# Second attention one step earlier: the next tile's projections and relay move forward by a step, and the first half's logits go in front of the second half's transposes

## The chip, the core and the metric

One core of a Trainium2 chip runs the whole program: TensorE (PE; its weight loads are listed apart as PEld), VectorE (DVE), ScalarE (ACT), GpSimd (POOL) and SyncE (SP), and 16 DMA engines that all queues share. The metric is the device time of one execution in microseconds (us), lower is better; a few runs are taken and their median is compared. The span is the part of an execution that the hardware profiler covers.

## The reference, cut to what matters

Two layers on 1024 tokens of width 512. Each is an attention, a residual with layer norm, a feed-forward part, and again a residual with layer norm. The change touches the second attention and the start of the last feed-forward part (its expert logits).

```python
x = _layernorm(x + _L0_attn_ref(x, ...))            # attention over the heads of one token
x = _layernorm(x + _L0_ffn_ref(x, ...))             # three layers of +1/-1 weights
# _L1_attn_ref: 32 heads of 16, a window of 128 keys, rotary embedding
q = (x @ Wq.T).reshape(B, S, 32, 16); k = _split_kv(x @ Wk.T); v = _split_kv(x @ Wv.T)
q = q * cos + rotate_half(q) * sin
k = k * cos + rotate_half(k) * sin
scores = einsum('bhqd,bhkd->bhqk', q, k) / 4
scores = where((j <= i) & (j > i - 128), scores, -inf)
out = einsum('bhqk,bhkd->bhqd', softmax(scores), v)
x = _layernorm(x + out @ Wo.T)
# _L1_ffn_ref: the top 2 of 16 experts by these logits, and a shared expert
logits = x2 @ gate_w.T
x = _layernorm(x + moe_out + shared_out)
```

## The kernel before, in words

Five programs, one per engine, are written out by hand and run in order on their engines; semaphores tie them together. The 1024 tokens are 8 tiles of 128. A float32 product is made of three matmuls of rounded halves (`split_terms`), so a projection of one tile is 12 matmuls with 512 columns.

**PSUM rings.** `Ring` (line 46) hands out banks in a fixed order: `fill` waits until the bank's former content has been released, `take` and `drained` wait for a filling and for its release. In the second attention V (two banks) holds the scores by rows, Q (two) the scores by keys, R (two) the projections and the output product, and U has one bank alone (line 213) for everything that is transposed in between: x2 (the input), turned (rotated K or Q), mx (the row maxima), context2 and co. So each filling of U waits until the one before it has been read by its last reader.

**The second attention** is a loop over i from -1 to 7 with eight steps s each. At step s three tiles are in work: r = i+1 has its scores by rows made on PE (`row_scores`) and their masked maxima taken on VectorE (`row_maxima`, four instructions of line 1184 per step); i has its scores by keys made (`key_scores`), exponentiated on ScalarE (`weights_out`), masked on GpSimd (`mask`, lines 1818 and 1821) and weighed with the values on PE (`weigh`, line 601); and t = i+2 is projected. d = i-1 gets its context transposed (`context_rows`, line 546), divided (`context_divided`), transposed again (`turn_context`, line 553) and multiplied with the output weights (`output`, in thirds at steps 5, 6 and 7), and `add_output` adds it to X.

**The projections of tile t before the change.** Step 0: K (`project2(t, 1)`, twelve matmuls of line 515). Step 1: Q, then the maxima of tile i's second half of heads are transposed (`turn_maxima(i, 1)`, line 539); VectorE in that step takes the row maxima, divides the context, rotates K (`rotate` and `rope_sum`, line 914), and then copies the maxima out (`maxima_out`). Step 2: the rotated K is transposed (`turn_rotated(t, 1)`, line 533), a third of V is made, and VectorE rotates Q. Step 3: the rest of V, and the rotated Q is transposed. Step 6: the input of the next tile is transposed (`turn_x`, line 508).

**The relay.** `parts_out_high` (ScalarE) and `parts_low` (VectorE) make the two rounded parts of rotated K and Q; SyncE writes them to DRAM (`relay_rows`, line 865) and GpSimd loads them back in another layout (`stack_rows`, line 1803, K in step 4 and Q in step 5). `row_scores(r, 0)` waits for both loads of tile r. `stack_maxima` (line 1810) puts the maxima beside them by a DMA, and `key_scores(i, 0, 0)` waits for it. After the last tile's relay SyncE loads the first shared-expert weights (`load_shared`, line 853), two of 768 KB, and a table.

**The passage.** After the loop the last tile's output is made, the tiles are normalised on ScalarE (`normalise`), transposed on PE (`turn_x3`, V ring, line 343), split by ScalarE and VectorE (`high_x3`, `low_x3`), and multiplied with the gate weights in two halves of four tiles (12 matmuls of line 332 each), copied out on VectorE (line 1314), and turned to logits by tokens, on which the choice of experts rests. The shared expert's products follow.

```python
                    if s < 2 and 2 <= t < T:
                        project2(t, 1 - s)
                    if s == 1 and i >= 0:
                        turn_maxima(i, 1)
```

Of the kernel before, what the change touches and what calls it, by code (L numbers as in the profile page):

```python
# [16 lines left out]
D = 512  # L17
DC = D // P
T = 1024 // P
G = 4  # L20
# [3 lines left out]
E = 16  # L24
# [55 lines left out]
def build(nc, x, wq, wk, wv, bias, k0, k1, k2, s0, s1, s2, aq, ak, av, ao, gate, experts, shared,  # L80
          rope_c, factor_c, table_c, out, xs, ys):
    with ExitStack() as ctx:
# [81 lines left out]
        co = FP[:, 13440:13952]  # L164
# [163 lines left out]
        def _(pe):  # L328
# [190 lines left out]
            def project2(t, n, at=0, count=3 * DC):  # L519

                if at == 0:
                    U.drained(pe, ("x2", t))
                    if n == 2:
                        pe.wait_ge(w_split, 4)
                    else:
                        pe.wait_ge(kq_split, (8, 4)[n])
                part_of(R, ("qkv", t, n), split_terms(turned_parts(x2T[t]), chunks(wsplit((1, 2, 0).index(n)))), at, count)
# [107 lines left out]
            for i in range(-1, T):  # L635
                t, r, d = i + 2, i + 1, i - 1
                for s in range(8):
# [6 lines left out]
                    if s < 2 and 2 <= t < T:  # L644
                        project2(t, 1 - s)
                    if s == 1 and i >= 0:
                        turn_maxima(i, 1)
                    if s == 2 and 2 <= t < T:
                        turn_rotated(t, 1)
                        project2(t, 2, 0, DC)  # L650
                    if s == 3 and 2 <= t < T:
                        project2(t, 2, DC, 2 * DC)
                        turn_rotated(t, 0)
                    if s == 4 and d >= 0:
                        turn_context(U, U, d)
# [14 lines left out]
                    if s == 6 and 2 <= t < T - 1:  # L670
                        turn_x(t + 1)
                    if s == 7 and d >= 0:
                        output(U, R, d, 2 * DC, DC)
                    if i >= 0 and s in (3, 5, 7):
                        weigh(i, s // 2 - 1)
# [14 lines left out]
            turn_x3(*range(2, T - 1))  # L690


# [3 lines left out]
            for g in range(2):  # L696
                if g == 1:
                    turn_x3(T - 1)
                V.drained(pe, ("x3", g * G + G - 1))
                x3 = [[XT3[g][:, a, c, :] for c in range(DC)] for a in range(2)]  # L700
                b = V.fill(pe, ("logitsT", g))
                product(b[0:E, :], split_terms([[gr[:, a, c, :] for c in range(DC)] for a in range(2)], x3)).then_inc(V.full, 1)
# [201 lines left out]
        def _(v):  # L904
# [343 lines left out]
            for i in range(-1, T):  # L1248
                t, r, d = i + 2, i + 1, i - 1
                for s in range(8):  # L1250
# [4 lines left out]
                    if s == 1 and 2 <= t < T:  # L1255
                        rotate(t, 1)
                        rope_sum(t, 1)
                    if s == 1 and i >= 0:
                        maxima_out(i, 1)
                    if s == 2 and 2 <= t < T:  # L1260
                        parts_low(t, 1)
                        rotate(t, 0)
                        rope_sum(t, 0)
                    if s == 3 and r < T:
                        maxima_split(r, 0)
                    if (i, s) == (-1, 3):
                        low_dense(("x2", 2), xa[2][1], xa[2][0])
                    if s == 3 and 2 <= t < T:
                        parts_low(t, 0)
# [8 lines left out]
                    if s == 6 and 2 <= t < T - 1:  # L1278
                        low_dense(("x2", t + 1), xa[t + 1][1], xa[t + 1][0])
# [21 lines left out]
            nc.vector.memset(picked[:, T, :], 0.0).then_inc(picked_ready, 1)  # L1301
            low_x3(0, 1)
            add_output(R, T - 1)
            low_x3(2, 3, 4)
            rates(slice(T - 1, T), 6)
            low_x3(5, 6)
            shared_low(2)


            for g in range(2):  # L1310
                if g == 1:
                    low_x3(T - 1)
                b = V.take(v, ("logitsT", g))
                nc.vector.tensor_copy(lgT[:, g * D:(g + 1) * D], b[0:E, :]).then_inc(V.free, 1)
# [132 lines left out]
        def _(s):  # L1447
# [190 lines left out]
            for i in range(-1, T):  # L1638
                t, d = i + 2, i - 1
                for step in range(8):  # L1640
                    if step == 0 and d >= 0:
                        context_out(d, 1)
                    if i >= 0 and (step % 2 == 0 or i >= 1):
                        weights_out(i, 2 * (step // 2), step % 2)
                    if step == 2 and 2 <= t < T:
                        parts_out_high(t, 1)
                    if step == 3 and 2 <= t < T:
                        values_out(t, ("qkv", t, 0))
                        parts_out_high(t, 0)
                    if step == 4 and d >= 0:  # L1650
                        high_dense(("co", d), coT[:, 0])
# [13 lines left out]
                    if step == 6 and 2 <= t < T - 1:  # L1665
                        high_dense(("x2", t + 1), x2T[t + 1][:, 0])
# [8 lines left out]
            roots(slice(0, T - 1), 5)  # L1675
            s.wait_ge(offset_ready, 6)
            normalise(0)
            normalise(1)
            high_dense(("co", T - 1), coT[:, 0])
            for t in range(2, T - 1):  # L1680
                normalise(t)
                high_x3(t - 2)
# [3 lines left out]
            high_x3(T - 3)  # L1686
            high_x3(T - 2)
            high_x3(T - 1)
# [38 lines left out]
        def _(p):  # L1727
# [103 lines left out]
            for i in range(-1, T):  # L1831
                t, r = i + 2, i + 1
                for step in range(8):
# [7 lines left out]
                    if step == 2 and i >= 0:  # L1841
                        stack_maxima(i, 1)
                    if step == 4 and 2 <= t < T:
                        stack_rows(t, 1)
                    if step == 5 and 2 <= t < T:
                        stack_rows(t, 0)
# [78 lines left out]
```

## Time and profile before

| what | value |
|---|---|
| three runs | 734.14, 737.02, 726.03 us |
| median of the runs | 734.14 us |
| the profiled execution | 728.87 us |
| its span | 727.1 us |
| mean granted clock of TensorE, share of full speed | 0.911 |
| busy share: PE, PEld, DVE, ACT, POOL | 85, 66, 54, 37, 33% |

The profiled execution took 1.8 us beyond its span and lies 5.3 us under the median of the runs. All times in the rows below are from its span's start. In the timeline's rows the columns are the start, the time until the group's end, the engine, the line, the operation with its target and sources, the count, and in brackets how long the engine sat idle before it and what ended that. "issue" is an idle stretch whose end the profile puts down to nothing it shows; waits on a DMA's semaphore come out so in part.

### The profile page before, as it was taken

The page shows a single profiled execution, that of the slowest core. Times are in us where ns is not written, and L with a number is a line of the kernel's source. Part 1 is how long each engine was busy: PE and PEld are TensorE (multiplying, and loading weights), DVE is VectorE, ACT ScalarE, POOL GpSimd, SP SyncE. Part 2 cuts the span into 40 slices and gives each one's busy share as a digit, 9 for nine tenths or more (in the row PEclk, how much of TensorE's full clock was granted, in tenths as well). Part 3 has the DMA queues.
Part 4 walks back from the last instruction along what each step waited for, and adds up shares of the span by engine and source line. Part 5 has one row for each costly group of instructions (what it writes and reads, how often), then busy time and mean ns, then how long its engine had stood idle before and what let it go on. Part 6 is the DMA issues. An engine that isn't in the chain of part 4 may idle for free.

```text
span 727.1 us, 13453 instructions
## 1 busy us (share of the span) xinstructions
PE 616.0 (85%) x5108; PEld 482.4 (66%) x5108; DVE 393.3 (54%) x1126; ACT 270.3 (37%) x433; POOL 238.9 (33%) x348
## 2 busy tenths in 40 slices
PE   2998999669889787989989895868789799999984
PEld 2987976557667555666767673645458688888761
DVE  4325445697765774757777484552554243323264
ACT  5155045366654223334344342444430122221213
POOL 6002523543410245535444452362007311111071
PEclk9999999889999885999999897577799899999997
DMA  8921211342056425536272648020007759998465
GB/s 293 394 115 31 52 33 26 104 134 74 0 139 150 119 96 81 132 46 159 45 152 89 88 119 156 2 89 2 1 1 283 270 209 416 418 417 292 168 165 182
DMA packets 49455, 104.37 MB, mean 144 GB/s; under 512 B 12208, under 2 KB 18480, under 8 KB 47856
## 3 DMA queue, kind: packets, MB, share of 16 engines
q1 hardware_dynamic: 30032, 61.68, 24.0%
q0 software_dynamic: 13744, 31.61, 19.3%
q10 hardware_dynamic: 5616, 10.23, 3.9%
q8 instruction: 41, 0.67, 0.4%
q14 instruction: 22, 0.18, 0.1%
HBM read 63.77 MB, written 35.13 MB: 136 GB/s over the span
## 4 chain that ended last, share of the span: by engine, by line
PE 62%; DVE 10%; ACT 9%; issue 7%; DMA 7%; POOL 4%; SPq 1%; POOLq 0%; ACTq 0%; DVEq 0%
PE bank L332 20%; PE bank L515 10%; PE bank L368 9%; ACT FP L1451 4%; DVE FP L914 3%; PE bank L601 3%; PE bank L586 3%; PE bank L573 3%; DMA QS<-QS 2%; PE bank L750 2%; POOL FP L1866 2%; PE bank L716 2%; PE bank L391 2%; PE bank L546 1%; PE bank L379 1%
## 5 line engine op out<-in xcount | busy, mean ns | idle before, releaser
L1451 ACT ACTIVATE FP<-bank 128x512 f32<-128x512 f32 (+1 forms) x244 | 138.6, 611 | 311.3 <-PE bank L586 128.6
L1184 DVE CUSTOM_DVE_ANT_0 kraw<-bank,maskb 128x256 bf16<-128x256 f32 (+1 forms) x256 | 88.5, 401 | 58.0 <-PE bank L573 58.0
L515 PE MATMUL bank<-W,XR 128*128 128x512 f32 x348 | 104.1, 444 | 0.2
L332 PE MATMUL bank<-FP 128*128 128x128 f32 x558 | 87.3, 311 | 0.8 <-ACT FP L1451 0.8
L368 PE MATMUL bank<-W,XR 128*128 128x512 f32 x288 | 76.6, 415 | 5.2 <-DVE W L914 5.2
L515 PEld LDWEIGHTS bank<-W,XR 128*128 128x128 f32 x348 | 69.4, 211 | 16.0 <-DVE XR L914 0.8
L1818 POOL TENSOR_SCALAR_AFFINE_SELECT FP<-FP 128x512 f32<-128x512 f32 x64 | 41.4, 669 | 114.8 <-ACT FP L1451 114.8
L368 PEld LDWEIGHTS bank<-W,XR 128*128 128x128 f32 x288 | 63.7, 271 | 11.3 <-DVE W L914 5.6
L332 PEld LDWEIGHTS bank<-FP 128*128 128x128 f32 x558 | 65.1, 192 | 2.8 <-DVE FP L914 1.6
L332 PE MATMUL bank<-RP,W 128*128 128x512 f32 x192 | 48.8, 413 | 5.0 <-issue 2.8
L914 DVE TENSOR_TENSOR FP<-FP,bank 128x128 f32<-128x128 f32 (+1 forms) x39 | 14.4, 369 | 70.5 <-ACT FP L1451 44.9
L332 PEld LDWEIGHTS bank<-RP,W 128*128 128x128 f32 x192 | 37.8, 199 | 14.5 <-issue 5.1
L1821 POOL TENSOR_SCALAR_AFFINE_SELECT FP<-FP 128x512 f32<-128x512 f32 x56 | 38.0, 704 | 24.5 <-ACT FP L1451 24.3
L1774 POOL DMA_DIRECT2D RPF<-FP x64 | 31.6, 501 | 39.7 <-PE bank L404 28.8
L1859 POOL DMA_DIRECT2D FP<-slots_in x31 | 16.7, 540 | 84.7 <-PE bank L716 77.8
L573 PE MATMUL bank<-RP,QS 48*128 48x256 f32 x160 | 23.7, 377 | 21.0 <-issue 10.0
L601 PE MATMUL bank<-FP 128*17 128x128 f32 x960 | 39.5, 318 | 2.1 <-ACT FP L1451 1.8
L1386 DVE COPY FP<-bank 128x512 f32<-128x512 f32 x31 | 21.4, 691 | 33.2 <-PE bank L716 33.2
L914 DVE TENSOR_TENSOR XR<-bank,XR 128x512 fp32r<-128x512 f32 x27 | 21.3, 807 | 32.4 <-ACT XR L1451 32.4
L601 PEld LDWEIGHTS bank<-FP 128*17 128x17 f32 x960 | 27.5, 111 | 14.2 <-issue 6.0
L573 PEld LDWEIGHTS bank<-RP,QS 48*128 48x128 f32 x160 | 14.7, 221 | 32.6 <-issue 23.4
L1854 POOL DMA_INDIRECT slots_in<-X,slots x16 | 16.6, 1037 | 48.6 <-issue 48.6
(168 smaller groups left out, 1019.1 us busy)
## 6 DMA issues: line engine op xcount, KB each, us to landing
FP<-in_experts_dram SPq DMA_DIRECT2D x31, 768.0 KB, 6.6
slots_out<-QS SPq DMA_DIRECT2D x48, 256.0 KB, 2.6
FP<-slots_in POOLq DMA_DIRECT2D x31, 256.0 KB, 6.6
slots_out<-FP ACTq DMA_DIRECT2D x31, 256.0 KB, 7.7
slots_in<-RP SPq DMA_DIRECT2D x7, 1024.0 KB, 13.1
RP<-slots_out POOLq DMA_DIRECT2D x16, 384.0 KB, 5.7
QS<-slots_out POOLq DMA_DIRECT2D x10, 384.0 KB, 8.3
FP<-in_shared_dram SPq DMA_DIRECT2D x4, 768.0 KB, 8.0
```

What stands on the lines that cost most here:

```text
L332: mm = nc.tensor.matmul(bank, lhs, rhs, start=(n == 0), stop=(n == len(terms) - 1))
L368: mm = nc.tensor.matmul(b[:, :], *terms[m], start=(m == 0), stop=(m == 3 * DC - 1))
L515: mm = nc.tensor.matmul(b[:, :], *terms[n], start=(n == 0), stop=(n == len(terms) - 1))
L573: mm = nc.tensor.matmul(both[a][:, m, :], qS[i % 3][half(a, 3 * HD), pr, :], kS[half(a, 3 * HD), slots, pr, :], start=True, stop=True)
L586: mm = nc.tensor.matmul(both[a][:, m * P:(m + 1) * P], kS[half(a, 3 * HD + 2), (i - w) % 4, pr, :], qS[i % 3][half(a, 3 * HD + 2), pr, :], ...
L601: mm = nc.tensor.matmul(weighing[32 * q:32 * q + HD + 1, (h // 4 % 4) * P:(h // 4 % 4 + 1) * P], vaug[:, (i - w) % 4, head(h), :], PT[hg % ...
L914: return nc.vector.tensor_tensor(o, a, b, op)
L1184: ins = nc.vector.tensor_tensor_reduce(masked[:, 2 * (f % 2) + m, 0:n], b[:, m, :], maskb[:, m0:m0 + n], 1.0, -BIG, ALU.add, ALU.max, hmax ...
L1451: return nc.scalar.activation(o, i, func, **kw)
L1774: nc.gpsimd.dma_start(vdiag[k % 3][32 * g:32 * g + 32, 272 * g:272 * g + 272].rearrange("p (s d) -> p s d", s=CH), vT[32 * g:32 * g + 32, ...
L1818: ins = nc.gpsimd.affine_select(out=pt, in_=pt, compare_op=ALU.is_ge, fill=0.0, base=0, pattern=[[0, 4], [1, P]], channel_multiplier=-1)
L1821: ins = nc.gpsimd.affine_select(out=pt, in_=pt, compare_op=ALU.is_ge, fill=0.0, base=-1, pattern=[[0, 4], [-1, P]], channel_multiplier=1)
```

## The change

The loop's iteration count and all operations stay; their order on each engine changes.

- K of the next tile (`project2(t + 1, 1)`) is made in step 7 of the iteration before, behind the output's last third and ahead of `weigh`; Q of tile t in step 0; V in steps 1 and 2; rotated K is transposed in step 1 and rotated Q in step 2; `turn_x(t + 1)` moves from step 6 to step 3.
- `turn_maxima(i, 1)` moves to the end of step 0 on PE. On VectorE `maxima_out(i, 1)` comes in step 0 ahead of `rotate(t, 1)` and `rope_sum(t, 1)`; before it came in step 1 behind them. Rotation of Q and the low parts move one step forward.
- ScalarE: the high parts and V's copy move one step forward, the high part of x2 from step 6 to 3. GpSimd: `stack_rows` in steps 3 and 4, `stack_maxima(i, 1)` in step 1.
- Passage: the logits of the first four tiles come behind the transposes of tiles 2 and 3, and the transposes of tiles 4 to 7 all behind them. On ScalarE the high part of the last context goes ahead of the wait for the offsets, and the high parts of tiles 4 to 7 all behind the last `normalise`. On VectorE the first logits' copy comes ahead of the low parts of tiles 4 to 7, and the second's behind `shared_low(2)`.

```diff
 (TensorE)
-                    if s < 2 and 2 <= t < T:
-                        project2(t, 1 - s)
-                    if s == 1 and i >= 0:
+                    if s == 0 and 2 <= t < T:
+                        project2(t, 0)
+                    if s == 0 and i >= 0:
                         turn_maxima(i, 1)
-                    if s == 2 and 2 <= t < T:
+                    if s == 1 and 2 <= t < T:
                         turn_rotated(t, 1)
                         project2(t, 2, 0, DC)
-                    if s == 3 and 2 <= t < T:
+                    if s == 2 and 2 <= t < T:
                         project2(t, 2, DC, 2 * DC)
                         turn_rotated(t, 0)
+                    if s == 3 and 2 <= t < T - 1:
+                        turn_x(t + 1)
...
-                    if s == 6 and 2 <= t < T - 1:
-                        turn_x(t + 1)
                     if s == 7 and d >= 0:
                         output(U, R, d, 2 * DC, DC)
+                    if s == 7 and 1 <= t < T - 1:
+                        project2(t + 1, 1)
...
-            turn_x3(*range(2, T - 1))
-            acc = banks[4:8]
-            pe.wait_ge(gate_ready, 2)
-            for g in range(2):
-                if g == 1:
-                    turn_x3(T - 1)
+            turn_x3(2, 3)
+            def logits_turned(g):
                 V.drained(pe, ("x3", g * G + G - 1))
...
+            logits_turned(0)
+            turn_x3(*range(G, T))
+            logits_turned(1)
 (VectorE)
-                    if s == 1 and 2 <= t < T:
+                    if s == 0 and i >= 0:
+                        maxima_out(i, 1)
+                    if s == 0 and 2 <= t < T:
                         rotate(t, 1)
                         rope_sum(t, 1)
-                    if s == 1 and i >= 0:
-                        maxima_out(i, 1)
-                    if s == 2 and 2 <= t < T:
+                    if s == 1 and 2 <= t < T:
                         parts_low(t, 1)
                         rotate(t, 0)
                         rope_sum(t, 0)
+                    if s == 2 and 2 <= t < T:
+                        parts_low(t, 0)
...
-                    if s == 3 and 2 <= t < T:
-                        parts_low(t, 0)
+                    if s == 3 and 2 <= t < T - 1:
+                        low_dense(("x2", t + 1), xa[t + 1][1], xa[t + 1][0])
...
-            low_x3(2, 3, 4)
+            low_x3(2, 3)
             rates(slice(T - 1, T), 6)
-            low_x3(5, 6)
+            logits_out(0)
+            low_x3(*range(G, T))
             shared_low(2)
...
+            logits_out(1)
 (ScalarE)
+                    if step == 1 and 2 <= t < T:
+                        parts_out_high(t, 1)
                     if step == 2 and 2 <= t < T:
-                        parts_out_high(t, 1)
-                    if step == 3 and 2 <= t < T:
                         values_out(t, ("qkv", t, 0))
                         parts_out_high(t, 0)
+                    if step == 3 and 2 <= t < T - 1:
+                        high_dense(("x2", t + 1), x2T[t + 1][:, 0])
...
+            high_dense(("co", T - 1), coT[:, 0])
             s.wait_ge(offset_ready, 6)
             normalise(0)
-            normalise(1)
-            high_dense(("co", T - 1), coT[:, 0])
-            for t in range(2, T - 1):
+            for t in range(1, G + 1):
                 normalise(t)
-                high_x3(t - 2)
+                high_x3(t - 1)
+            for t in range(G + 1, T - 1):
+                normalise(t)
...
-            high_x3(T - 3)
-            high_x3(T - 2)
-            high_x3(T - 1)
+            for t in range(G, T):
+                high_x3(t)
 (GpSimd)
-                    if step == 2 and i >= 0:
+                    if step == 1 and i >= 0:
                         stack_maxima(i, 1)
+                    if step == 3 and 2 <= t < T:
+                        stack_rows(t, 1)
                     if step == 4 and 2 <= t < T:
-                        stack_rows(t, 1)
-                    if step == 5 and 2 <= t < T:
                         stack_rows(t, 0)
```

## Rows read from the trace of the kernel before

**Rows 1.** The page's chain that ended last, by engine.
```profile
PE 62%; DVE 10%; ACT 9%; issue 7%; DMA 7%; POOL 4%; SPq 1%; POOLq 0%; ACTq 0%; DVEq 0%
```

**Rows 2.** Windows, loop iterations i = 0 to 5: length, engines' busy us, PEclk, DMA share.
```profile
250.87:282.90 32.03, 24.27 (x178) 17.78 (x179) 20.55 (x83) 12.65 (x19) 15.44 (x18) 0.71 0.50 100
282.90:316.34 33.44, 29.97 (x298) 23.05 (x299) 22.40 (x91) 12.48 (x23) 14.77 (x24) 0.88 0.50 97
316.34:349.58 33.24, 29.74 (x298) 22.54 (x299) 22.42 (x91) 12.48 (x23) 14.71 (x24) 0.90 0.46 97
349.58:379.51 29.93, 28.04 (x298) 21.29 (x299) 21.81 (x90) 12.12 (x23) 14.74 (x24) 0.94 0.49 108
379.51:411.23 31.72, 28.20 (x300) 21.35 (x300) 22.87 (x93) 12.83 (x24) 14.74 (x24) 0.95 0.50 102
411.23:450.14 38.91, 27.92 (x294) 21.18 (x295) 22.76 (x90) 11.96 (x22) 14.72 (x24) 0.88 0.59 128
```

**Rows 3.** Timeline of PE, iteration i = 3.
```profile
349.58 0.51 PE L573 MATMUL bank<-RP,QS 48*128 48x256 f32 x4 [1.29 <-issue]
...
350.94 3.01 PE L515 MATMUL bank<-W,XR 128*128 128x512 f32 x12
...
355.12 3.01 PE L515 MATMUL bank<-W,XR 128*128 128x512 f32 x12
357.96 0.27 PE L539 MATMUL bank<-ident,FP 128*32 128x128 f32 x1
...
359.20 0.63 PE L533 MATMUL bank<-ident,FP 128*128 128x128 f32 x4
...
363.96 0.65 PE L533 MATMUL bank<-ident,FP 128*128 128x128 f32 x4 [0.32 <-DVE FP L914]
...
365.54 0.51 PE L573 MATMUL bank<-RP,QS 48*128 48x256 f32 x4
...
367.74 0.50 PE L573 MATMUL bank<-RP,QS 48*128 48x256 f32 x4 [0.71 <-DVE hmax L1184]
```

**Rows 4.** Timeline of VectorE, the first steps of iteration i = 3.
```profile
350.09 0.42 DVE L1184 CUSTOM_DVE_ANT_0 kraw<-bank,maskb 128x256 bf16<-128x256 f32 x1 [0.96 <-PE bank L573]
...
351.76 0.49 DVE L914 TENSOR_TENSOR FP<-bank,hsum 128x128 f32<-128x128 f32 x2
...
356.49 1.34 DVE L914 TENSOR_TENSOR FP<-bank,rope 128x512 f32<-128x512 f32 x3
357.87 1.10 DVE L914 TENSOR_TENSOR FP<-FP 128x512 f32<-128x512 f32 x1
```

**Rows 5.** Timeline of PE, the starts of iterations 1, 5 and 6.
```profile
282.90 0.80 PE L573 MATMUL bank<-RP,QS 48*128 48x256 f32 x4 [3.23 <-DMA QS<-slots_out]
...
411.23 0.50 PE L573 MATMUL bank<-RP,XR 48*128 48x256 f32 x4 [1.24 <-issue]
412.51 0.66 PE L586 MATMUL bank<-QS,RP 50*128 50x128 f32 x8 [0.78 <-DMA QS<-QS]
...
413.51 4.58 PE L515 MATMUL bank<-W,XR 128*128 128x512 f32 x12
...
450.14 0.80 PE L573 MATMUL bank<-RP,QS 48*128 48x256 f32 x4 [8.39 <-issue]
```

**Rows 6.** Timeline of SyncE and GpSimd: the last tile's relay and the first shared weights.
```profile
433.23 1.20 SPq L853 DMA_DIRECT2D FP<-in_shared_dram  x2
...
434.73 1.05 POOL L1803 DMA_DIRECT2D QS<-slots_out  x2
```

**Rows 7.** Timeline of the passage, ScalarE and PE.
```profile
507.65 1.52 ACT L1451 ACTIVATE X<-X,offset,rstd 128x512 f32<-128x512 f32 x2 [0.47 <-DVE offset L1045]
...
521.52 5.12 PE L332 MATMUL bank<-RP,XR 128*16 128x512 f32 x12 [1.63 <-DVE RP L914]
526.48 0.60 PE L343 MATMUL bank<-ident,X 128*128 128x128 f32 x4
528.56 2.95 PE L332 MATMUL bank<-RP,XR 128*16 128x512 f32 x12 [1.48 <-DVE RP L914]
```

More of the change, by code:

```diff
@@ L702, in _ @@
                 product(b[0:E, :], split_terms([[gr[:, a, c, :] for c in range(DC)] for a in range(2)], x3)).then_inc(V.full, 1)
+            acc = banks[4:8]
+            pe.wait_ge(gate_ready, 2)
+            logits_turned(0)
+            turn_x3(*range(G, T))
+            logits_turned(1)
             V.drained(pe, ("logitsT", 1))
@@ L1277, in _ @@
                         rates(slice(G, T), 4)
-                    if s == 6 and 2 <= t < T - 1:
-                        low_dense(("x2", t + 1), xa[t + 1][1], xa[t + 1][0])
                     if s == 7 and r < T:
@@ L1301, in _, with logits_out @@
             nc.vector.memset(picked[:, T, :], 0.0).then_inc(picked_ready, 1)
+            def logits_out(g):
+                b = V.take(v, ("logitsT", g))
+                nc.vector.tensor_copy(lgT[:, g * D:(g + 1) * D], b[0:E, :]).then_inc(V.free, 1)
             low_x3(0, 1)
             add_output(R, T - 1)
-            low_x3(2, 3, 4)
+            low_x3(2, 3)
             rates(slice(T - 1, T), 6)
-            low_x3(5, 6)
+            logits_out(0)
+            low_x3(*range(G, T))
             shared_low(2)
[L1310 to L1314, printed above, removed]
+            logits_out(1)
             def spread(vec, axis, shape):
@@ L1664, in _ @@
                         context_out(i, 0)
-                    if step == 6 and 2 <= t < T - 1:
-                        high_dense(("x2", t + 1), x2T[t + 1][:, 0])
                     if i == T - 2 and step in (2, 5):
```

## The prediction

> **What bounds the kernel now.** I read the page's chain first: PE carries 62% of it, "issue" and DMA 14% together [rows 1]. So PE's own work sets the time, with waits in it. Then the table of windows, one per iteration of the second attention: iterations 1 to 4 do the same work and take 33.44, 33.24, 29.93 and 31.72 us, together 128.3, with PE busy for 28.0 to 30.0 of each and VectorE for about 22 [rows 2]. VectorE is not full, but it has an order. Iteration 0 takes 32.03 and iteration 5 takes 38.91.
>
> Then the timeline of PE. At the starts of iterations PE waits for the relayed rows: 3.23 us at iteration 1, 1.29 at 3, 1.24 at 5 and 8.39 at 6, and once more 0.78 for the maxima beside them [rows 3, 5]. These the change is aimed at. Behind the 1.24 and 0.78 the twelve matmuls of a projection take 4.58 us in place of 3.01 [rows 3, 5]: part of them runs at 1.2 GHz, half of TensorE's clock, as twelve in the passage do in full, in 5.12 [rows 7]. In iteration 0 the granted clock is 0.71 of full speed in the mean [rows 2].
>
> **The loop, iterations 1 to 4.** No instruction is added or removed; each queue is reordered. Take iteration 3 as the pattern and count from its `row_scores(r, 0)` at 349.58 [rows 3]. Before, PE makes K and Q (3.0 each) and only then transposes rotated K, at 359.20, 9.6 us in. VectorE, though, rotates K at 356.49, beside the Q projection at 355.12, and is done with the sum at 358.97, just ahead of PE [rows 3, 4].
>
> After the change K is already there, and PE reaches the transposition of rotated K sooner: row and key scores and context rows take 1.4 us (K began at 350.94) [rows 3], Q 2.9, the maxima 0.2, the next scores and context rows 1.25 (355.12 less 350.94 and 2.9), so 5.7 us in. But two waits in the new order hold it there:
> - VectorE copies the maxima out ahead of rotating K. PE transposes these maxima behind Q's projection, so at 4.3 to 4.6, and VectorE, done with its context division at 2.7 (351.76 plus 0.49, less 349.58) [rows 4], stands still until then. Copy 0.3: 4.9. Rotation and sum 2.4 (356.49 to 358.97) [rows 4]: 7.3.
> - The transposition's bank in U must be free, and U has one bank, which then holds the second context half. VectorE divides that in step 1 behind `row_maxima` (350.09 to 351.47, where the division begins: 1.4) and takes 0.8 for it (to 352.25) [rows 4]. 7.3 + 1.4 + 0.8 = 9.5.
>
> So PE waits some 3.8 us, and transposes rotated K at 9.55, the same time as before (9.6). What the earlier K saved is gone, and what was put behind is net. From there:
> - Rotated Q's transposition follows at +4.76 as before (359.20 to 363.96) [rows 3], the chain through ScalarE, `parts_low` and rotation being the same.
> - Before, step 4 began at +6.34 (365.54) [rows 3]. Now a `row_scores` stands between, and it waits for `row_maxima` of the step before it, which VectorE only takes behind the sum (1.4 us, to about +6.0); then row and key scores 0.85, `turn_x` 0.4 (it needs the low part of Q, to +6.85), `weigh` 1.0: step 4 begins at +8.35, 2.0 later.
> - If PE runs some 4 us at half clock after the 3.8 us wait, Q's transposition is late by 1.7 and step 4 begins at about +10.0, 3.7 later. The 4.58 us row stands behind waits of 2.0 together, 1.6 us above full clock, while the 1.29 us wait of iteration 3 has a full-clock projection behind it [rows 3, 5]; so I take the patch to happen in half of the tiles: 2.85.
> - Step 4 to 5 is held by VectorE as before (the 0.71 at 367.74 [rows 3]), with x2's low part in it: +0.2.
> - Step 6 loses `turn_x`, 0.5. Step 7 gains K's projection, 3.0.
> - The wait at the iteration's start goes: K's 3 us lies over the relay and the maxima's DMA. In iteration 3 it is worth 0.3 + 0.7 = 1.0.
>
> 29.93 + 2.85 + 0.2 - 0.5 + 3.0 - 1.0 = 34.5, and 33.6 to 35.3 by the two cases; I take 34.3, as iteration 3 has one slow patch of its own at step 5 that can overlap. Four of these are 137.2, against 128.3: +8.9 (bounds +5.7 and +12.5). The start waits and the slow projections behind them, which make the others of the four longer than iteration 3, are counted in the 128.3.
>
> **Iterations -1 and 0.** K of tile 2 now runs at the end of -1, where PE would wait for VectorE anyway; of its 3.0 us (or 5.1 at half clock [rows 3, 7]) I take 0.3 to 2.2 to stick out, an estimate that sets it against a wait of the size of those at iteration starts (up to 3.23) [rows 5]. In iteration 0 there is no context: rotated K can be transposed at 7.3, for the second of the two waits is absent, in place of 9.6 or later at its low clock, the later steps lose about 2.5 to `row_maxima`, `turn_x` and the like, step 7 gains 3.0, and the 3.23 us wait at 282.90 [rows 5] goes: about -1.5 in all. With what -1 adds I take 0, with bounds -4 and +2.
>
> **Iteration 5 and the last relay.** No further K and no `turn_x`, so PE is through its steps after about 31 us. The last Q load was issued at 434.73, 23.5 us in, 1.5 us behind the start of the shared weights' load at 433.23 [rows 6], and PE got it at 450.14, 15.4 us after issue [rows 5, 6]. The weights' load waits only for the relay's writes, so it moves forward with them: the writes end at about 20 in place of 22, GpSimd's Q load goes at 21.5 and lands at 36.9. That is -2.0 against 38.91; bounds 0 and -8. The second bound is nearly the whole wait of 8.39 gone [rows 5].
>
> The DMA queues bear on this. The Trainium skill, DMA: Bandwidth & Descriptors, section Issuing engines are not separate DMA queues, says that transfers from SyncE and GpSimd share the 16 engines and interleave. By that rule the Q load stays slow as long as it is issued behind the weights' load; the 15.4 us agree, and it speaks against the rival that has the wait gone.
>
> **Iterations 6 and 7.** The maxima go one step forward on engines that wait for each other there anyway: 0, bounds -1 and +1.
>
> **The passage.** Before, the first logits ran at 521.52, at half clock (5.12 us for twelve), tile 7's transposition was stuck behind them until 526.48, and the second logits began 2.1 us after it [rows 7]. After: `normalise(0)` comes behind the context's high part, and so some 2 us later than 507.65 [rows 7]; tile 1's transposition stands ahead of the output product on PE, so that moves by +1.5. The first logits need two tiles fewer and start about 1.9 us earlier even so, at 519.6. But now four transpositions, splits and low parts lie behind them in place of one: 5.7 us in place of 1.9. -1.9 + 3.8 = +1.9. At full clock the first logits take 2.95 and the sum is -0.3; PE is as lightly loaded ahead of them as before, so I take +1.8, bounds -1 and +3. This shifts all that follows.
>
> **Sum.** 0 + 8.9 - 2.0 + 0 + 1.8 = +8.7. On the profiled execution's own 728.87 that is 737.6. It lies 5.3 below the median of the runs, which spread over 11; on the median the same sum is 742.8. I name 739.
>
> **Rivals.**
> - *The aim is met* (faster). The place is the transposition of rotated K: if it starts within 6 us of the iteration's start, iterations take 29.93 less 1.0, 28.9, four of them 115.7 or -12.6; iteration 0 gains 3, iteration 5 gains 2, the passage costs 1.8: 713. For it speaks that VectorE has 8 us idle in every iteration [rows 2] and that the start waits are real [rows 5]; against it, that VectorE takes its instructions in order and U has one bank. I would have to have misread one of these.
> - *The last relay wins* (no change). The loop is longer, but the last K and Q loads slip ahead of the shared weights: -8 in place of -2, so 731.6. For it: K's load goes a step earlier and Q's is only 1.5 us behind [rows 6]. Against: the load of the weights moves with them.
> - *The clock* (slower by over 2%). If the 3.8 us wait costs half clock in every tile (+12.5 in place of +8.9) and the patch reaches a further group of twelve (5.1 in place of 3.0, +8 over four tiles) [rows 3, 7]: 749. It decides from a mean granted clock under 0.85 in iterations 1 to 4, where it was 0.88 to 0.95 [rows 2]. The Trainium skill, TensorE: Matmul & The Clock Gate, section HAM oscillation, tells of a loop that waits once per pass and restarts at the low clock in every pass; by that it would happen in each tile. The trace agrees for the 3.23 us wait and not for the 1.29 us one, so it bears on a new 3.8 us wait.
>
> **How the numbers follow.** My forecast 0.50, the aim met 0.13, the last relay 0.17, the clock 0.20. A measurement of this kernel tells about 2% from no change, here 14.7 us: under 719.5 or over 748.8. All of the aim met and a little of the relay case is faster: 0.14. Half of the clock case and the top of the forecast's own bounds is slower: 0.18. The rest, 0.68, within. The range for eight in ten leaves most of the first rival out below and reaches past the clock's 749 above, with the 5.2 us between profile and median: 721 to 756.
>
> **What would show it.** In the changed profile, iterations 1 to 4 of about 34 us, with no wait at their starts; a wait of PE of 3 to 4 us at line 533 in each, released by VectorE's context division; VectorE idle ahead of the maxima's copy; a wait of about 1 us at `row_scores` of step 3; iteration 5 at about 37 with a wait of 5 or 6 at its end; the second logits some 2 us later against the loop's end. Iterations under 31 us would make the prediction wrong, and so would the last relay's wait under 2 us.

## The result, and the profile after

The changed kernel takes 749.06 us (median of 4 runs, 746.54 to 749.95) against 734.92 before (726.03 to 737.02): a ratio of 1.0217, with a 95% interval from 1.0172 to 1.0261. It is slower by 14.1 us, or 2.2%; the interval reaches to both sides of 2%, so only that it is slower is settled, not that it is so by more than 2%. The forecast was 739, within a range of 721 to 756: the direction and the range hold, the size is too small. The profiled execution is the one of 748.2 us, with a span of 746.4, which is 19.3 over the span before. Medians in this text are over all runs of a kernel, while the ratios leave out executions that were longer at a lower granted clock than the others, such as the profiled one of `late_shared` (721.02 us), from whose trace no length is taken.

The table of windows for the same iterations, 0 to 5 (length, busy us of PE, PEld, DVE, ACT and POOL with their counts, granted clock, DMA share, GB/s):

```profile
252.41:283.27 30.86, 23.12 (x180) 17.07 (x180) 24.09 (x80) 10.85 (x17) 15.40 (x18) 0.78 0.48 105
283.27:321.22 37.95, 31.60 (x298) 24.42 (x298) 24.40 (x93) 11.95 (x22) 15.03 (x25) 0.82 0.35 85
321.22:356.19 34.97, 29.14 (x302) 22.42 (x298) 23.76 (x91) 12.55 (x23) 14.84 (x24) 0.90 0.43 93
356.19:393.74 37.55, 31.80 (x304) 24.37 (x300) 23.77 (x91) 12.66 (x23) 14.66 (x24) 0.82 0.41 86
393.74:431.27 37.53, 31.78 (x303) 24.35 (x299) 23.77 (x91) 12.65 (x23) 14.65 (x24) 0.82 0.38 86
431.27:470.03 38.76, 29.01 (x287) 21.69 (x283) 23.26 (x90) 12.65 (x23) 14.66 (x24) 0.82 0.56 128
```

Iterations 1 to 4 take 148.0 us where they took 128.3 [rows 2]: +19.7, which is the whole loss. The others come to little: iterations -1 and 0 together +0.4 (iteration 1 starts at 283.27 in place of 282.90), iteration 5 -0.2, iterations 6 and 7 -0.6, the passage -0.5, what follows it +0.5. PE's busy time grows too, in iteration 3 from 28.04 us [rows 2] to 31.80, with the same matmuls: they are slower.

PE in iteration 3, in the timeline; the rows to set beside it are [rows 3]:

```profile
356.19 0.50 PE L573 MATMUL bank<-RP,QS 48*128 48x256 f32 x4
...
357.44 3.01 PE L515 MATMUL bank<-W,XR 128*128 128x512 f32 x12
360.29 0.27 PE L539 MATMUL bank<-ident,FP 128*32 128x128 f32 x1
...
361.32 0.66 PE L546 MATMUL bank<-ident,FP 128*128 128x128 f32 x4
365.78 1.09 PE L533 MATMUL bank<-ident,FP 128*128 128x128 f32 x4 [3.80 <-DVE FP L917]
366.51 2.05 PE L515 MATMUL bank<-W,XR 128*128 128x512 f32 x4
...
369.97 3.78 PE L515 MATMUL bank<-W,XR 128*128 128x512 f32 x8
373.55 1.05 PE L533 MATMUL bank<-ident,FP 128*128 128x128 f32 x4
...
376.18 0.63 PE L508 MATMUL bank<-ident,X 128*128 128x128 f32 x4 [0.72 <-DVE QS L917]
...
377.74 0.50 PE L573 MATMUL bank<-RP,QS 48*128 48x256 f32 x4
```

The iteration starts without a wait, as the change wants. Then PE stands still for 3.80 us ahead of rotated K's transposition, which begins 9.59 us into the iteration; before, it was 9.6. Behind the wait the matmuls take nearly twice as long: four of 512 columns 2.05 us in place of 1.17, eight 3.78 in place of 2.1, and the transposition of rotated Q at 373.55 takes 1.05 in place of 0.65. A window from 365.78 to 373.60 gives a granted clock of 0.50, which is 1.2 GHz, and so does one from 373.60 to 374.50; from 374.75 on it is 1.00. Step 4 begins 12.0 us behind the transposition of rotated K, where it was 6.3.

VectorE in the same stretch:

```profile
358.40 0.49 DVE L917 TENSOR_TENSOR FP<-bank,hsum 128x128 f32<-128x128 f32 x2
360.59 0.28 DVE L1201 CAST QS<-bank 32x128 fp32r<-32x128 f32 x1 [1.70 <-PE bank L539]
360.80 1.33 DVE L917 TENSOR_TENSOR FP<-bank,rope 128x512 f32<-128x512 f32 x3
362.17 1.48 DVE L917 TENSOR_TENSOR FP<-FP 128x512 f32<-128x512 f32 x1
...
365.14 0.49 DVE L917 TENSOR_TENSOR FP<-bank,hsum 128x128 f32<-128x128 f32 x2
```

It has divided the first context half at 358.9, then waits 1.70 us for PE's transposed maxima (behind Q's projection), copies them at 360.59, and only then rotates K. The row maxima and the division of the second half follow to 365.6; the U bank is free and PE goes on at 365.78. PE, idle from 362.0, waited for a chain that had itself waited for PE.

The last relay, from all engines' timeline and from PE's:

```profile
454.19 0.82 SPq L856 DMA_DIRECT2D FP<-in_shared_dram  x2
...
455.44 1.04 POOL L1805 DMA_DIRECT2D QS<-slots_out  x2
```
```profile
470.03 0.67 PE L573 MATMUL bank<-RP,QS 48*128 48x256 f32 x4 [3.53 <-issue]
```

The weights' load has moved forward with the relay, as [rows 6] had it 1.5 us ahead of Q's load, now 1.25. Q is there 14.6 us after its issue (15.4 before). The wait is 3.53 us in place of 8.39, but because PE arrives later.

The passage on PE:

```profile
531.33 4.73 PE L515 MATMUL bank<-W,XR 128*128 128x512 f32 x12
...
539.21 2.95 PE L332 MATMUL bank<-RP,XR 128*16 128x512 f32 x12 [2.28 <-DVE RP L917]
...
545.22 0.63 PE L343 MATMUL bank<-ident,X 128*128 128x128 f32 x4 [0.42 <-DVE RP L917]
547.33 2.94 PE L332 MATMUL bank<-RP,XR 128*16 128x512 f32 x12 [1.48 <-DVE RP L917]
```

The output product is slower here (4.73 us in place of 4.03), and the first logits run at full clock, in 2.95 where they took 5.12 [rows 7]. From the last half of the context rows (524.93) to the second logits (547.33) it is 22.40 us; before it was 22.94.

### The profile page after: what moved, and what is told of

Read it like the earlier page. It is cut to its first block, busy times and chain, and to the rows that moved or that the text cites. A ratio compares the mean times of both kernels' runs of the same rounds, so it can differ in the third digit from the quotient of the medians.

```text
span 746.4 us, 13454 instructions
## 1 busy us (share of the span) xinstructions
PE 625.4 (84%) x5108; PEld 493.2 (66%) x5108; DVE 403.6 (54%) x1126; ACT 271.5 (36%) x433; POOL 239.2 (32%) x348
## 4 chain that ended last, share of the span: by engine, by line
PE 61%; DVE 12%; ACT 8%; DMA 7%; issue 6%; POOL 5%; SPq 1%; POOLq 0%; ACTq 0%; DVEq 0%
PE bank L332 16%; PE bank L515 14%; PE bank L368 9%; DVE FP L917 4%; PE bank L601 4%; ACT FP L1453 3%; PE bank L586 3%; PE bank L573 2%; POOL slots_in L1856 2%; PE bank L719 2%; POOL FP L1868 2%; DVE kraw L1187 2%; PE bank L391 2%; PE bank L533 1%; PE bank L379 1%
## 5 line engine op out<-in xcount | busy, mean ns | idle before, releaser
L515 PE MATMUL bank<-W,XR 128*128 128x512 f32 x348 | 114.2, 480 | 0.2
L332 PE MATMUL bank<-FP 128*128 128x128 f32 x558 | 88.9, 315 | 0.8 <-ACT FP L1453 0.8
L515 PEld LDWEIGHTS bank<-W,XR 128*128 128x128 f32 x348 | 76.5, 231 | 17.9 <-DVE XR L917 0.3
L368 PE MATMUL bank<-W,XR 128*128 128x512 f32 x288 | 77.5, 419 | 5.2 <-DVE W L917 5.2
L368 PEld LDWEIGHTS bank<-W,XR 128*128 128x128 f32 x288 | 64.2, 271 | 11.8 <-DVE W L917 5.6
L332 PEld LDWEIGHTS bank<-FP 128*128 128x128 f32 x558 | 66.8, 196 | 2.6 <-DVE FP L917 1.6
L332 PE MATMUL bank<-RP,W 128*128 128x512 f32 x192 | 45.7, 394 | 2.2 <-DVE FP L917 2.2
L332 PEld LDWEIGHTS bank<-RP,W 128*128 128x128 f32 x192 | 35.8, 188 | 10.5 <-issue 1.9
L601 PEld LDWEIGHTS bank<-FP 128*17 128x17 f32 x960 | 27.3, 110 | 11.6 <-POOL FP L1823 4.8
L533 PE MATMUL bank<-ident,FP 128*128 128x128 f32 x64 | 14.0, 360 | 21.9 <-DVE FP L917 21.9
```

Of the source, the lines that this page charges most:

```text
L332: mm = nc.tensor.matmul(bank, lhs, rhs, start=(n == 0), stop=(n == len(terms) - 1))
L368: mm = nc.tensor.matmul(b[:, :], *terms[m], start=(m == 0), stop=(m == 3 * DC - 1))
L515: mm = nc.tensor.matmul(b[:, :], *terms[n], start=(n == 0), stop=(n == len(terms) - 1))
L601: mm = nc.tensor.matmul(weighing[32 * q:32 * q + HD + 1, (h // 4 % 4) * P:(h // 4 % 4 + 1) * P], vaug[:, (i - w) % 4, head(h), :], PT[hg % ...
```

## The experiments

My theory after the result: the loss is made in the loop by VectorE's order at the first two steps, through a wait of PE at rotated K, and most of it is the half clock behind that wait. Rivals: K's 3 us in step 7 are the loss, and the wait only takes up slack; or the passage shares in it. Ratios are against the kernel before, which was run again beside each set of experiments, with medians from 731.63 to 735.07 us. So a difference between medians of two sets is uncertain by some 3 us.

**Loop and passage apart.** `loop_only` is the changed kernel with the passage of before (its other lines on VectorE and ScalarE put back too), `passage_only` the kernel before with the new passage.

```diff
 (loop_only, against the changed kernel)
-            turn_x3(2, 3)
+            turn_x3(*range(2, T - 1))
...
```

> The changed loop with the passage of before. Theory (the loss is in the loop, the passage is neutral or gains the 0.5 us that the two traces show between the last context rows and the second logits): 749 to 750 us, within 1 us of the changed kernel. Rival (the passage costs the 1.8 us that I had forecast): 747 us, and the stretch from the last context rows to the second logits is shorter than the 22.4 us of the changed kernel.

> The kernel before with only the new passage. Theory: the stretch from the second half of the last context rows to the second logits is 22.4 us in place of 22.9, so 0.5 us faster than before, not to be told from no change. Rival (my forecast, +1.8 us): 24.7 us.

`loop_only` took 747.59 us (ratio 1.0208, 1.0142 to 1.0273), `passage_only` 732.37 (0.9949, 0.9902 to 0.9997). The stretch from the context rows' second half to the second logits is 22.79 us in `loop_only` (527.77 to 550.56) and 22.43 in `passage_only` (509.52 to 531.95), against 22.94 before and 22.40 after. So the passage gains 0.4 to 0.5 us in the traces, not the 1.8 lost that I forecast. By the time alone `loop_only` fits the rival's 747, but the rival wanted a stretch shorter than 22.4 us, and it is 22.79. By the runs the passage can't be told from nothing in the one case and may be slightly faster in the other. The loop has the loss.

**K's rotation ahead of the maxima's copy.** Only two blocks of the changed kernel swap places on VectorE.

```diff
+                    if s == 0 and 2 <= t < T:
+                        rotate(t, 1)
+                        rope_sum(t, 1)
                     if s == 0 and i >= 0:
                         maxima_out(i, 1)
-                    if s == 0 and 2 <= t < T:
-                        rotate(t, 1)
-                        rope_sum(t, 1)
```

> The changed kernel, with K's rotation ahead of the maxima's copy on VectorE in step 0 (nothing else). Theory (VectorE's standstill ahead of the copy holds the rotation): rotated K is transposed 7.6 us into the iteration in place of 9.6, PE's wait there falls from 3.8 to about 1.9 us, and the iteration from 37.5 to 35.5, or to 33.6 where the half clock goes too: 739 down to 730 us. Rival (K's projection in step 7 is the loss, and the wait only takes the slack of the later chain): the time moves to the wait for rotated Q, iterations stay at 37, 748 us.

It took 719.82 us, ratio 0.9777 (0.9696 to 0.9859): 29 us faster than the changed kernel, and faster than the kernel before. Three of its windows, iterations 1, 3 and 4, and PE in iteration 4 and then in iteration 5:

```profile
279.51:316.49 36.98, 32.60 (x298) 24.96 (x298) 24.36 (x93) 11.95 (x22) 14.55 (x25) 0.82 0.37 87
346.91:377.31 30.40, 26.57 (x304) 20.63 (x300) 23.86 (x91) 12.55 (x23) 14.65 (x24) 1.00 0.49 107
377.31:409.14 31.83, 28.01 (x303) 21.43 (x300) 23.85 (x91) 12.55 (x23) 14.71 (x24) 0.95 0.48 101
```
```profile
384.69 0.63 PE L533 MATMUL bank<-ident,FP 128*128 128x128 f32 x4 [1.43 <-DVE FP L917]
385.07 1.17 PE L515 MATMUL bank<-W,XR 128*128 128x512 f32 x4
...
387.01 2.12 PE L515 MATMUL bank<-W,XR 128*128 128x512 f32 x8
...
416.52 0.63 PE L533 MATMUL bank<-ident,FP 128*128 128x128 f32 x4 [1.43 <-DVE FP L917]
416.90 1.86 PE L515 MATMUL bank<-W,XR 128*128 128x512 f32 x4
...
420.17 3.78 PE L515 MATMUL bank<-W,XR 128*128 128x512 f32 x8
```

Rotated K is transposed 7.4 us into the iteration, the wait is 1.43 us, and in iterations 2 to 4 the matmuls behind it run at full clock. In iteration 5 the same wait of 1.43 us is followed by half clock: eight matmuls take 3.78 us. In iteration 1 PE also waits at the start, 0.97 and 1.00 us, and Q's projection behind that runs at half clock, in 5.12 us, as do the first matmuls behind its wait of 1.35 us for rotated K; the iteration takes 36.98 us, nearly as long as in the changed kernel. Iterations of 30.4 and 31.8 in place of 37.5 are less than theory's 33.6; in iterations 2 and 3 the clock also stays up at step 5. The rival falls: K's projection is in step 7 here as well.

**The wait kept, PE busy in it.** The changed kernel with twelve extra matmuls ahead of rotated K's transposition, into V's bank, which the real ones overwrite. (In this kernel the first third of V's terms is made with K's weights, so V's values are others; number and size of its matmuls are those of V.)

```diff
                     if s == 1 and 2 <= t < T:
+                        b = R.fill(pe, ("qkv", t, 2))
+                        for _ in range(12):
+                            nc.tensor.matmul(b[:, :], *first, start=True, stop=True)
                         turn_rotated(t, 1)
```

> The changed kernel with twelve extra matmuls of V's first term on PE in the wait ahead of rotated K's transposition; their result is overwritten. The wait's end stays where it is, but PE is busy in it. Theory (about half of the loop's loss is the half clock behind the wait): V's two thirds take 2.1 us in place of 3.8, iterations go from 37.5 to about 34.2, and the kernel to about 737 us in spite of 3 us more of matmuls per tile. Rival (the wait itself is the loss and the clock falls anyway): iterations stay at 37.5, 749 us or a little more.

It took 734.42 us, ratio 1.0044 (1.0004 to 1.0084): 14.6 us faster than the changed kernel, with 72 matmuls more. Iteration 3, by its window and on PE:

```profile
354.47:387.05 32.58, 29.52 (x315) 22.79 (x311) 24.35 (x91) 12.55 (x23) 15.42 (x24) 1.00 0.47 99
```
```profile
360.47 3.01 PE L652 MATMUL bank<-W,XR 128*128 128x512 f32 x12 [0.21 <-DVE FP L923]
364.07 0.63 PE L533 MATMUL bank<-ident,FP 128*128 128x128 f32 x4 [0.59 <-DVE FP L923]
364.45 1.17 PE L656 MATMUL bank<-W,XR 128*128 128x512 f32 x4
...
366.38 2.11 PE L515 MATMUL bank<-W,XR 128*128 128x512 f32 x8
...
372.62 0.50 PE L573 MATMUL bank<-RP,QS 48*128 48x256 f32 x4
```

Rotated K is transposed at 9.60 us (364.07 less 354.47), the same as in the changed kernel, so VectorE's chain is untouched. What differs is the clock, 1.00 in place of 0.82, and the iteration, 32.58 in place of 37.55. Step 4 begins 8.55 us behind the transposition, where the forecast without the half clock had 8.35 and the changed kernel has 11.96. So of the 5.0 us that the half clock costs in iteration 3, 3.4 lie behind the wait. The other 1.6 lie at step 5 (5.72 us from step 4 to step 6 in place of 7.28), and that stretch the kernel before had too (7.29), so it is no part of the loss. Taken against 8.55 in the same way, the half clock behind the wait comes to 10.7 us over iterations 1 to 4, of the 19.7 lost. The wait's own length is worth 2.2 us more: `rotate_first`, also at full clock in iteration 3, takes 30.40. And 32.58, with no half clock at all, is still 0.5 over the mean of 32.1 before, which had some.

**The wait made longer again.** The kernel with the rotation first, and the rotation's first multiply on VectorE done three times more.

```diff
+                if n == 1 and t >= 2:
+                    for _ in range(3):
+                        own(tt(r, b, cos, ALU.mult))
                 tt(r, b, cos, ALU.mult).then_inc(turned_halves, 1)
```

> As the run with K's rotation first (720 us), with the first multiply of K's rotation done three times more on VectorE, about 2.2 us, so that PE's wait for rotated K is 3.6 us again, at another order. Theory (behind a wait of this length PE runs at half clock, behind 1.4 us it does not): iterations go from 30.4 to 36 or 37 us, 745 us. Rival (the clock fell for another reason, the order or the lower load of PE): iterations 32.6 us at full clock, 733 us.

It took 733.78 us, ratio 0.9968 (0.9921 to 1.0015): 14 us over `rotate_first`, and between the two expectations, nearer the rival's in total. The trace says why:

```profile
356.48 1.09 PE L546 MATMUL bank<-ident,FP 128*128 128x128 f32 x4 [2.51 <-DVE QS L1204]
358.54 1.09 PE L533 MATMUL bank<-ident,FP 128*128 128x128 f32 x4 [0.97 <-DVE FP L917]
359.28 2.05 PE L515 MATMUL bank<-W,XR 128*128 128x512 f32 x4
...
362.67 2.14 PE L515 MATMUL bank<-W,XR 128*128 128x512 f32 x8
```
```profile
348.77:382.93 34.16, 28.57 (x302) 22.37 (x298) 25.53 (x94) 12.56 (x23) 14.70 (x24) 0.90 0.47 95
```

The wait came in two pieces, 2.51 and 0.97 us, with four transpositions between. PE did run at half clock behind the first piece, in iterations 2 to 4 alike, but was back before 362.67, 6 us later; in iteration 3 of the changed kernel it took 8.8. These iterations take 34.1 us: over the 30.4 of `rotate_first`, 2.4 are the later transposition (9.77 us into the iteration in place of 7.39) and 1.4 the way from there to step 4 (9.95 in place of 8.56), which the clock makes longer. So the half clock comes back with the wait, and my price of 36 to 37 us, taken from the changed kernel's patch, is refuted. Neither whether a patch comes nor how long it lasts follows from the wait's length alone, as iterations 4 and 5 of `rotate_first` show with 1.43 us each.

**K alone.** The kernel before, with only K's projection in step 7 of the iteration before.

```diff
-                    if s < 2 and 2 <= t < T:
-                        project2(t, 1 - s)
+                    if s == 1 and 2 <= t < T:
+                        project2(t, 0)
...
+                    if s == 7 and 1 <= t < T - 1:
+                        project2(t + 1, 1)
```

> The kernel before, with only K's projection moved into step 7 of the iteration before. Theory (early K by itself is near neutral; the order on VectorE is the loss): rotated K is transposed 7.6 us into the iteration in place of 9.6, the waits at the iterations' starts go, 3 us of K come in step 7: iterations of 31 to 32 us, 728 to 736 us. Rival (K in step 7 is what costs, with its 3 us on the path behind the maxima): iterations of 34 us or more, 742 us.

It took 717.63 us, ratio 0.9798 (0.9733 to 0.9864), better than the theory's 728 to 736. Iterations 2 to 4, and PE at the start of iteration 6:

```profile
314.16:345.29 31.13, 28.27 (x304) 21.60 (x300) 22.77 (x91) 12.47 (x23) 14.00 (x24) 0.95 0.50 104
345.29:374.42 29.13, 26.36 (x302) 20.66 (x299) 22.28 (x91) 12.97 (x24) 14.78 (x24) 1.00 0.57 111
374.42:406.63 32.21, 29.81 (x298) 22.91 (x298) 23.02 (x91) 12.00 (x23) 14.00 (x24) 0.89 0.46 100
```
```profile
440.04 0.80 PE L573 MATMUL bank<-RP,QS 48*128 48x256 f32 x4 [7.51 <-issue]
```

The waits at the starts of iterations 1 to 5 are gone but for 0.55 us at one of them. The wait at the start of iteration 6 is still 7.51 us, but it begins sooner: iteration 5 takes 33.41 us in place of 38.91, and iterations 1 to 4 together 120.9 in place of 128.3. So early K is a gain of some 2% by itself, and what the change adds to it turned that into a loss. `rotate_first` keeps all of those additions but the maxima's copy ahead of the rotation, and takes 719.82 us. So the copy's place is nearly all of it, and moving the other steps forward as well gained nothing that the runs show.

**The U bank freed sooner, and the last relay.** `rotate_divide_first` is `rotate_first` with the division of the second context half ahead of the row maxima in step 1. `late_shared` adds one wait on SyncE, and `before_late` puts that wait alone into the kernel before.

```diff
 (rotate_divide_first, against rotate_first)
-                    if r < T:
+                    if r < T and s != 1:
                         row_maxima(r, s)
                     if s < 2 and d >= 0:
                         context_divided(U, d, s)
+                    if r < T and s == 1:
+                        row_maxima(r, s)
 (late_shared, against rotate_divide_first; before_late, against the kernel before)
             sp.wait_ge(parts_out[0], 48 * T)
+            sp.wait_ge(stack_in[0][1], 32 * (T // 2))
             load_shared(0)
```

> As the run with K's rotation first, and on VectorE in step 1 the context's division ahead of the row maxima (the U bank is free 1.4 us sooner). Theory (the wait at rotated K is VectorE's order): the 1.43 us wait there goes to zero, rotated K is transposed 6 us into the iteration in place of 7.4, and iterations fall from 30.4 to 29 to 30 us: 712 to 718 us. Rival (only the clock counted, and at full clock the wait's place does not matter): the 1.4 us come back at the wait for rotated Q or at the row scores of step 3, iterations stay at 30.4, 719 us.

> As rotate_divide_first, and SyncE's first shared-weight loads wait until the last tile's Q is back from DRAM. Theory (the last Q load is slow because the 1.5 MB of shared weights share its DMA engines): the wait at the start of iteration 6, 3.96 us in the run with the rotation first, falls under 1 us, and the kernel gains 3 to 4 us on rotate_divide_first: 709 to 715 us. Rival (the load is late by itself): the wait stays at 4 us, and the later weights hold ScalarE in iteration 6: same or slower than rotate_divide_first.

> The kernel before, with only the first shared-weight loads held back until the last tile's Q is back from DRAM. Theory (the 8.39 us wait at the start of iteration 6 is the last Q load sharing the DMA engines with 1.5 MB of weights): the wait falls to the 1 to 3 us of the other tiles, and the kernel gains 4 to 7 us: 727 to 731 us. Rival (the load would be late anyway, or the weights then hold ScalarE in iteration 6): the wait stays over 6 us or comes back in iteration 6, and the time stays at 735 us.

`rotate_divide_first` took 717.48 us (0.9753, 0.9709 to 0.9797), so at best a little faster than `rotate_first`. Iterations 2 to 4 take 29.95, 31.44 and 29.87 us. The wait at rotated K falls from 1.43 to 0.97, not to zero. U now holds the maxima until VectorE has copied them, at 379.69, so PE's context rows come at 380.10 and their division at 381.06; iteration 4 on PE:

```profile
381.69 0.63 PE L533 MATMUL bank<-ident,FP 128*128 128x128 f32 x4 [0.96 <-DVE FP L917]
...
386.45 0.66 PE L533 MATMUL bank<-ident,FP 128*128 128x128 f32 x4 [0.32 <-DVE FP L917]
387.83 0.50 PE L573 MATMUL bank<-RP,QS 48*128 48x256 f32 x4 [0.73 <-DVE hmax L1187]
```

`late_shared` took 713.47 us (0.9683, 0.9634 to 0.9733), the fastest of all and within its expectation. `before_late` took 725.55 (0.9915, 0.9868 to 0.9961), a little better than its 727 to 731. Iteration 6 starts like this, first in `before_late`, then in `late_shared`:

```profile
448.28 0.50 PE L573 MATMUL bank<-RP,QS 48*128 48x256 f32 x4 [2.35 <-issue]
```
```profile
435.88 0.50 PE L573 MATMUL bank<-RP,QS 48*128 48x256 f32 x4
```

The wait of 8.39 us [rows 5] is 2.35 with the weights' load behind Q's, so about 6 us of it came from that load. Q is in use 9.4 us after its load was issued (438.90 to 448.28) in place of 15.4. In `late_shared` PE has no idle time there.

## Why the prediction was right, and where not

- *Rotated K's transposition.* Forecast: a wait of 3.8 us, the transposition at 9.55. Measured: 3.80, and 9.59. Both of its causes are shown: the copy's place by `rotate_first` (wait 1.43), the U bank by `rotate_divide_first` (0.97).
- *The way to step 4.* At full clock forecast +2.0, and `busy_wait` shows +2.2 (8.55 against 6.34). The term that was mis-sized is the half clock behind the wait: "If PE runs some 4 us at half clock after the 3.8 us wait", worth 1.7 us, and "I take the patch to happen in half of the tiles: 2.85". It happened in all four, and lasted 7.7, 2.7, 8.8 and 8.8 us: in iterations 1 to 4 step 4 begins 11.6, 9.4, 12.0 and 12.0 us behind the transposition, +4.9 in the mean. The forecast was 2.0 too small per iteration, 8 us in the four. I had sized the patch by the row of 4.58 us [rows 5], behind two waits of 2.0 us together; where it lasted 8.8 us it cost 3.4.
- *No wait at the iterations' starts.* Right for iterations 2 to 5. Iteration 1 still starts with a wait of 1.69 us, 0.50 more for the maxima, and Q's projection behind them at 4.58 us, so that rotated K is transposed 11.9 us in, 2.3 later than in the others. With the 8 and small differences these are the 10.8 us between +8.9 and +19.7.
- *A wait of about 1 us at the row scores of step 3.* It is not there in iteration 3 of the changed kernel, since the slow matmuls fill it; `busy_wait`, at full clock, has it with 0.73 us.
- *Iterations -1 and 0.* Forecast 0, measured +0.4.
- *Iteration 5.* Forecast 36.9 with a wait of 5 or 6 us, measured 38.76 with 3.53. The contention was right (14.6 us to landing, and `before_late`). The steps ahead of the Q load were late by their own half clock: it is issued 24.2 us in, not 21.5. The Trainium skill, DMA: Bandwidth & Descriptors, section Issuing engines are not separate DMA queues, says that transfers share the 16 DMA engines whichever engine starts them. The trace agrees: the Q load stayed slow behind SyncE's weights, against the rival of the last relay.
- *The passage.* Forecast +1.8, measured -0.5. "PE is as lightly loaded ahead of them as before, so I take +1.8" failed: the first logits ran at full clock, the case for which the text had -0.3. They do so in `passage_only` too (2.93 us), and in `loop_only`, with the passage of before, they take 5.08, so it belongs to the new order.
- *The sum.* The traces have +19.3 where it had +8.7. The loop's 10.8 are that difference; iteration 5 (1.9 too little) and the passage (2.3 too much) cancel by luck. That the range held is owed to its upper end, which was set to reach past the clock's 749.
- *The rivals.* The one on the clock had the size: its mark, a granted clock under 0.85, is met in three of the four iterations (0.82, 0.90, 0.82, 0.82), and its 749 is what was measured. It had the place wrong, since K's group in step 7 is not slower (twelve of its matmuls and four of the output product take 3.93 us at 388.01); the patch reaches through V and, in iterations 3 and 4, Q's transposition instead. The Trainium skill, TensorE: Matmul & The Clock Gate, section HAM oscillation, says that a loop with a wait in each pass restarts at the low clock in each; this trace agrees, in every iteration from 1 to 5, while in `rotate_first` iterations 2 to 4 have a wait of 1.43 us and no restart. I gave it 0.20 because a patch had followed only some of the waits before. None of the waits in rows 3 and 5 ahead of a projection was as long as 3.8 us, though.
- *The aim is met.* `rotate_first` shows that a gain was within reach of a swap of two blocks. `late_shared` comes to the price of 713, but by another sum: the rival had iterations of 28.9 us and rotated K transposed within 6.

Open is what makes the patch in the changed kernel last about 8 us in iterations 1, 3 and 4 and 2.7 in iteration 2, behind the same wait of 3.80, and what makes one follow the wait of 1.43 us in iteration 5 of `rotate_first` and not in iterations 2 to 4.

## What to carry to other kernels

When a producer's step is moved forward, follow every in-order queue that it passes: here one copy ahead of one rotation made VectorE wait for PE and PE for VectorE, and it cost more than the move could give. Price a new wait of TensorE with the clock behind it, and as a range: behind the same 3.8 us wait the half clock cost between 0.9 and 3.4 us. And where an urgent load shares its time with a bulk load that is not urgent, hold the bulk load back behind it.

## What the runs showed of the hardware that was not expected

- Twelve matmuls of no use in each of six tiles, 3.0 us for the twelve, made the kernel 14.6 us faster (734.42 against 749.06): TensorE stayed at 2.4 GHz behind them, with a granted clock of 1.00 in iterations 2 to 4 in place of 0.82 to 0.90.
- Behind the same wait of 3.80 us the half clock lasted from 365.78 to about 374.6 in iteration 3, and from 330.80 to about 333.5 in iteration 2. Behind 2.51 and 0.97 us with four transpositions between, it lasted about 6 us, the second wait included. Behind 1.43 us it came in one iteration of `rotate_first`, for some 7 us, and not in three others.
- A pair of loads of 384 KB each from DRAM took 14.6 us to be in use when issued 1.25 us behind the start of 1.5 MB of weights, and 15.4 in the kernel before. With the weights held back it took 9.4 (`before_late`).
